# Scores over three PSUM banks, row maxima one step ahead of the gate chunks, and half the value projection ahead of the last attend

## The reference

```python
# L0: attention with 16 heads of 16, then a SwiGLU layer, f32
a = gamma * rmsnorm(x) + beta
q, k, v = a @ W_q.T, a @ W_k.T, a @ W_v.T
attn = softmax(0.25 * q @ k.T); o = attn @ v
x = x + alpha * (o @ W_o.T)
h = gamma2 * rmsnorm(x) + beta2
x = x + alpha2 * (silu(h @ gate_w.T) * (h @ hidden_w.T) @ out_w.T + out_b)
# L1: gated MLP (1024), activations rounded to 8 bits by row, down_w to three values
u = (x * scale * rsqrt(mean(x * x))) @ up_w.T; val, gate = split(u)
x = x + act_quant(val * gelu(gate)) @ weight_quant(down_w).T
# L2: an adapter 256 -> 128 -> 256 whose weights a hyper network makes per sequence
x = x + relu(x @ Wd_b.T + bd) @ Wu_b.T + bu
# L3: layer norm, a per-sequence offset, weight and bias
```

## Time and profile before

| what | value |
|---|---|
| median of 3 runs | 1128.26 us (1128.12 to 1128.39) |
| the profiled execution | 1123.06 us, its span (first to last instruction) 1121.3 us |
| mean granted PE clock over the span | 0.960 |
| a full pass, as pass 8 | 61.9 us |

### The profile page before, as it was taken

The page is one execution under the profiler, slowest core; times in us unless marked ns, Lnnn a source line. Parts: engine busy times, 40 slices in busy tenths (PEclk is TensorE's granted clock), DMA queues, the critical chain, the costliest instruction groups (busy, mean ns, idle before and its releaser), DMA issues.

```text
span 1121.3 us, 22327 instructions
## 1 busy us (share of the span) xinstructions
PE 1006.8 (90%) x7426; PEld 850.9 (76%) x7426; DVE 752.4 (67%) x1711; ACT 553.2 (49%) x1144; POOL 193.1 (17%) x250
## 2 busy tenths in 40 slices
PE   5586789999999999999999999999999999997964
PEld 4245659697988879796979888797979788885952
DVE  4645547686777767776767677777867677776552
ACT  3154354655555454646555554646465545545430
POOL 1421601021120202010111202020201112020210
PEclk9578999999999999999999999999999999999995
DMA  8974622030404021120404040211304040300000
GB/s 292 296 294 133 250 91 66 22 113 2 133 1 127 5 91 41 49 83 6 126 1 132 1 122 10 81 51 39 93 1 132 1 132 1 113 11 10 11 19 9
DMA packets 78049, 89.45 MB, mean 80 GB/s; under 512 B 18672, under 2 KB 64640, under 8 KB 75392
## 3 DMA queue, kind: packets, MB, share of 16 engines
q1 hardware_dynamic: 72368, 63.86, 19.0%
q0 software_dynamic: 2304, 16.78, 4.1%
q10 hardware_dynamic: 3344, 8.39, 2.2%
HBM read 63.14 MB, written 25.31 MB: 79 GB/s over the span
## 4 chain that ended last, share of the span: by engine, by line
PE 69%; DVE 12%; DMA 6%; issue 5%; ACT 4%; SPq 2%; POOL 1%; DVEq 0%; ACTq 0%; POOLq 0%
PE bank L639 15%; PE bank L594 15%; PE bank L555 8%; PE bank L608 5%; PE bank L539 5%; PE bank L565 5%; PE bank L573 3%; DMA q_stack<-few_rows 3%; PE bank L500 2%; PE bank L671 2%; PE bank L657 2%; PE bank L677 1%; DVE den_x L1151 1%; DVE den_x L1153 1%; DVE o_norm L1155 1%
## 5 line engine op out<-in xcount | busy, mean ns | idle before, releaser
L1120 DVE TENSOR_REDUCE neg_max<-bank 128x2 f32<-128x512 f32 x256 | 164.8, 684 | 18.7 <-PE bank L539 18.7
L457 POOL TENSOR_TENSOR act_lo<-act_f,act_hi 128x256 fp32r<-128x256 f32 x128 | 94.4, 738 | 423.7 <-ACT act_hi L907 423.6
L865 ACT ACTIVATE probs<-bank 128x512 f32<-128x512 f32 x256 | 138.4, 593 | 57.1 <-PE bank L555 56.7
L901 ACT ACTIVATE silu_g<-bank 128x256 f32<-128x256 f32 x128 | 49.1, 384 | 183.5 <-PE bank L594 183.3
L555 PE MATMUL bank<-q_stack,k_stack 128*128 128x256 f32 x512 | 106.4, 324 | 9.6 <-DMA q_stack<-few_rows 6.4
L555 PEld LDWEIGHTS bank<-q_stack,k_stack 128*128 128x128 f32 x512 | 75.1, 195 | 50.0 <-ACT probs L865 30.9
L639 PE MATMUL bank<-up_hi,h_hi 128*128 128x256 f32 x512 | 108.0, 292 | 1.7 <-DVE y L1093 1.0
L944 ACT ACTIVATE gelu_g<-bank,r 128x256 f32<-128x256 f32 x128 | 60.7, 474 | 95.7 <-PE bank L639 94.8
L594 PE MATMUL bank<-h_hi,gh_hi 128*128 128x256 f32 x512 | 103.6, 284 | 4.6 <-DVE h_lo L1181 4.6
L594 PE MATMUL bank<-h_lo,gh_hi 128*128 128x256 f32 x512 | 103.4, 284 | 0.0
L639 PE MATMUL bank<-up_lo,h_hi 128*128 128x256 f32 x512 | 102.9, 282 | 0.0
(11 more groups left out here) (158 smaller groups left out, 2127.4 us busy)
## 6 DMA issues: line engine op xcount, KB each, us to landing
hyper<-w_hyper POOLq DMA_DIRECT2D x16, 1024.0 KB, 7.0
q_stack<-q_dram SPq DMA_DIRECT2D x96, 128.0 KB
k_stack<-k_dram SPq DMA_DIRECT2D x96, 128.0 KB
q_dram<-probs SPq DMA_DIRECT2D x16, 512.0 KB, 2.8
k_dram<-probs SPq DMA_DIRECT2D x16, 512.0 KB, 3.6
x_res<-xT SPq DMA_DIRECT2D x16, 256.0 KB, 2.8
out<-xc SPq DMA_DIRECT2D x16, 256.0 KB, 2.5
x_in<-xT SPq DMA_DIRECT2D x15, 256.0 KB, 2.8
```

The costliest lines, as they stand in the source:

```text
L457: pool.tensor_tensor(act_lo[:, c % 3, :], act_f[:, c % 2, :], act_hi[:, c % 3, :].bitcast(F32), ALU.subtract).then_inc(g_lo.sem, 1)
L865: act.activation(probs[:, h % SLOTS], halves(h % 2), ACT.Exp, scale=float(H / D) ** 0.5).then_inc(s_exp.sem, 1)
L1120: dve.tensor_reduce(neg_max[:, qt, :, pair:pair + 1].rearrange("p a o -> p (a o)"), halves(n % 3), AX_X, ALU.max, negate=True).then_inc(ma ...
```

## The change

1. The blocks of `max_scores` are given out by `maxima(c)`: three in step 0, two in each of steps 1 to 6, and the last one behind `ffn_out` in step 6. `max_turn` moves from step 8 to step 7, behind gate 7 and ahead of `ffn_out(f, 5)`. On DVE the reductions follow this, and the last stands ahead of the gated product of step 7. On ACT `max_row_out` moves ahead of the last `act_high`.
2. The scores use banks 0, 1 and 5 in turn, and a score waits for the exponential three heads back. The first three scores follow `mlp_down(g, 0)`, two more the second `mlp_down`, and two go ahead of and behind each `attend` from there; the last one stands alone. The small steps of `g` (`y_turn`, `adapter_down`, `adapter_up`) move from ahead of the scores of each turn to behind its `attend`. `norm_g` moves behind scores 3 and 4 and from bank 5 to bank 3, so the third `attend` waits for its end on DVE. On ACT `square_g` moves behind exponential 1 and `guess_g` from behind exponential 3 to behind 5. On DVE `norm_a(nxt)` goes ahead of `scaled_y(g)`.
3. `project_v(nxt, 0)` moves from behind `ln_var` to ahead of the last `attend`. It waits for `n1_dve` too.

```diff
@@ -33,6 +33,7 @@
 UW = F // UC
 BN = 128
 SLOTS = 7
+SCORE_BANKS = (0, 1, 5)
 NHY, HYW = 16, 2048
 MAGIC = 12582912.0
 EPS_RMS, EPS_LN = 1e-6, 1e-5
@@ -289,6 +290,10 @@
             run(Batch(NB - 1), Batch(NB - 2), Batch(NB - 3), None)
             run(None, Batch(NB - 1), Batch(NB - 2), None)
             run(None, None, Batch(NB - 1), None)
+
+        def maxima(c):
+
+            return range(0, 3) if c == 0 else range(2 * c + 1, 2 * c + 3)
 
         def starts(b):
 
@@ -516,6 +521,7 @@
                         mm.then_inc(done.sem, 1)
 
                 def project_v(b, t):
+                    pe.wait_ge(n1_dve.sem, n1_dve.at(b))
                     if t == 0 and b.follows():
                         pe.wait_ge(o_dve.sem, o_dve.at(b, 5, back=1))
                     for c in range(DC):
@@ -549,10 +555,10 @@
                     if h == 0:
                         pe.wait_ge(max_dma.sem, max_dma.at(b))
                         pe.wait_ge(max_row.sem, max_row.at(b))
-                    if h >= 2:
-                        pe.wait_ge(s_exp.sem, s_exp.at(b, h - 1))
+                    if h >= 3:
+                        pe.wait_ge(s_exp.sem, s_exp.at(b, h - 2))
                     for k in range(TT):
-                        mm = pe.matmul(halves(h % 2)[:, k, :], k_stack[:, h, k * P:(k + 1) * P], q_stack[:, h // 2, :],
+                        mm = pe.matmul(halves(SCORE_BANKS[h % 3])[:, k, :], k_stack[:, h, k * P:(k + 1) * P], q_stack[:, h // 2, :],
                                        start=True, stop=True)
                     mm.then_inc(s_mm.sem, 1)
 
@@ -615,7 +621,7 @@
                     pe.wait_ge(n3_act.sem, n3_act.at(b, 1))
                     for t in range(TT):
                         for c in range(DC):
-                            mm = pe.matmul(bank[5][:, t:t + 1], sq3[:, c, t * P:(t + 1) * P], mean_w[:, 0:1],
+                            mm = pe.matmul(bank[3][:, t:t + 1], sq3[:, c, t * P:(t + 1) * P], mean_w[:, 0:1],
                                            start=(c == 0), stop=(c == DC - 1))
                     mm.then_inc(n3_pe.sem, 1)
 
@@ -718,10 +724,10 @@
                             q_turn(g, 0)
                         if g and c == 6:
                             q_turn(g, 1)
-                        if a and c < FC:
-                            max_scores(a, 2 * c)
-                            max_scores(a, 2 * c + 1)
-                        if a and c == FC:
+                        if a and c < FC - 1:
+                            for n in maxima(c):
+                                max_scores(a, n)
+                        if a and c == FC - 1:
                             if starts(a):
                                 pe.wait_ge(small_in.sem, 16 * 6)
                             max_turn(a)
@@ -731,40 +737,43 @@
                             norm_a(nxt)
                         if f and c >= 2:
                             ffn_out(f, c - 2)
+                        if a and c == FC - 2:
+                            max_scores(a, 15)
                         if starts(a) and c in (7, 9):
                             hyper_product(c // 2 - 1)
                         if starts(f) and c in RUN1:
                             hyper_product(8 + RUN1.index(c))
                     if g:
                         mlp_down(g, 0)
-
                     if a:
-                        scores(a, 0)
-                        scores(a, 1)
+                        for h in range(0, 3):
+                            scores(a, h)
                     if g:
                         mlp_down(g, 1)
+                    if a:
+                        for h in range(3, 5):
+                            scores(a, h)
                     if f:
                         norm_g(f)
-                    if a:
-                        scores(a, 2)
-                        scores(a, 3)
                     for t in range(4):
-                        if g and t < 3:
-                            (y_turn, adapter_down, adapter_up)[t](g)
                         if a:
+                            if t == 2 and f:
+                                pe.wait_ge(n3_dve.sem, n3_dve.at(f))
                             if t < 3:
-                                scores(a, 4 * t + 4)
                                 scores(a, 4 * t + 5)
-                            if t == 2 and f:
-                                pe.wait_ge(x2_dve.sem, x2_dve.at(f))
+                                scores(a, 4 * t + 6)
+                            elif nxt:
+                                project_v(nxt, 0)
                             attend(a, t)
-                            if t < 3:
-                                scores(a, 4 * t + 6)
-                                scores(a, 4 * t + 7)
                         if starts(a):
                             hyper_product(4 + t)
                         if starts(f) and t >= 2:
                             hyper_product(12 + t)
+                        if g and t < 3:
+                            (y_turn, adapter_down, adapter_up)[t](g)
+                        if a:
+                            for h in range(4 * t + 7, min(4 * t + 9, H)):
+                                scores(a, h)
 
                     if nxt:
                         project_qk(nxt)
@@ -776,7 +785,7 @@
                         project(a)
                     if g:
                         ln_var(g)
-                    if nxt:
+                    if nxt and not a:
                         project_v(nxt, 0)
                     if a:
                         norm_f(a)
@@ -862,7 +871,7 @@
                         act.wait_ge(qk_dram_w.sem, qk_dram_w.at(b))
                     if h >= SLOTS:
                         act.wait_ge(pv_mm.sem, pv_mm.at(b, (h - SLOTS) // 4 + 1))
-                    act.activation(probs[:, h % SLOTS], halves(h % 2), ACT.Exp, scale=float(H / D) ** 0.5).then_inc(s_exp.sem, 1)
+                    act.activation(probs[:, h % SLOTS], halves(SCORE_BANKS[h % 3]), ACT.Exp, scale=float(H / D) ** 0.5).then_inc(s_exp.sem, 1)
 
                 def den_guess(b, u):
                     act.wait_ge(o_dve.sem, o_dve.at(b, 8 * u + 3))
@@ -916,7 +925,7 @@
                     act.wait_ge(n3_pe.sem, n3_pe.at(b))
                     if b.follows():
                         act.wait_ge(n3_dve.sem, n3_dve.at(b, back=1))
-                    act.activation(y3[:], bank[5][:, 0:TT], ACT.Ln, bias=eps_rms).then_inc(n3_act.sem, 1)
+                    act.activation(y3[:], bank[3][:, 0:TT], ACT.Ln, bias=eps_rms).then_inc(n3_act.sem, 1)
                     act.wait_ge(n3_act.sem, n3_act.at(b, 2))
                     act.activation(y3[:], y3[:], ACT.Exp, scale=-0.5).then_inc(n3_act.sem, 1)
 
@@ -993,17 +1002,15 @@
                             square_a(nxt)
                         if f and c == 2:
                             bias_x1(f)
+                        if a and c == FC:
+                            max_row_out(a)
                         if f and c >= 1:
                             act_high(f, c - 1)
                         if starts(f) and c in RUN1:
                             hyper_out_piece(8 + RUN1.index(c))
-                    if a:
-                        max_row_out(a)
                     act.preload_act_table_set("natural_log_exp_and_others")
                     if nxt:
                         guess_a(nxt)
-                    if f:
-                        square_g(f)
                     if starts(a):
                         hyper_out_piece(3)
                         raw_load(3)
@@ -1014,7 +1021,9 @@
                         for h in range(4 * t, 4 * t + 4):
                             if a:
                                 exps(a, h)
-                            if f and h == 3:
+                            if f and h == 1:
+                                square_g(f)
+                            if f and h == 5:
                                 guess_g(f)
                             if f and h == 9:
                                 hi_g(f)
@@ -1199,7 +1208,7 @@
                                                  ALU.mult, ALU.add).then_inc(x2_dve.sem, 1)
 
                 def norm_g(b):
-                    v = bank[5][:, 0:TT]
+                    v = bank[3][:, 0:TT]
                     dve.wait_ge(n3_act.sem, n3_act.at(b))
                     dve.scalar_tensor_tensor(v, v, EPS_RMS, y3[:], ALU.add, ALU.mult).then_inc(n3_dve.sem, 1)
                     dve.wait_ge(n3_dve.sem, n3_dve.at(b, 1))
@@ -1315,14 +1324,13 @@
                         dve.wait_ge(consts.sem, 6)
                         dve.wait_ge(ternary.sem, TERNARY)
                     for c in range(FC):
-                        if f and c < FC - 1:
+                        if a and c == FC - 1:
+                            row_max(a, 15)
+                        if f:
                             gated(f, c)
-                        if a:
-                            row_max(a, 2 * c)
```

(10 more changed lines are left out.)

## The result

The changed kernel takes 1105.05 us (median of 4 runs, 1103.09 to 1106.64) beside 1128.19 us before (4 runs): a ratio of 0.9831, 95% interval 0.9801 to 0.986. The prediction said 1097.6, between 1087 and 1112. Its profiled execution took 1104.08 us with a span of 1102.3; the span before was 1121.3. So 19.0 us went from the span, where the sum by steps had 30.7.

What follows compares the result with a forecast made beforehand. PE, busy 90% of the span, was taken to bound the kernel. 1.8 us in each of 14 full passes, 5 in pass 1 and 0.5 in pass 0 gave 30.7: 1092.4, plus 5.2 for the median: 1097.6, range 1087 to 1112.

Steps and rivals of the forecast that it cites:

- the sum by steps: Whole kernel: 1.8 us in each of 14 full passes, 5 in pass 1, 0.5 in pass 0, in all 30.7 us.
- two rivals: Third bank brings nothing (1108.8 us, chance 0.15); DVE's lag from the early maxima reaches gates and `ffn_out` (1111.6, chance 0.13).
- Maxima one step ahead: PE ahead of the row maxima's transposes and first scores: first scores start 1.0 us earlier a pass, bounds 0.5 to 1.1.
- The 0.95 at the transposes: PE hole ahead of the row maxima's transposes, waiting for the last score block's reduction; claimed to go, 0.95 us.
- Scores over three banks: Score stretch: last score starts 11.5 us after the first instead of 12.14, gaining 0.6 a pass, bounds 0 to 1.1.
- the shorter tail: End of the score stretch: last exponential ends 1.1 us after its score starts instead of 1.33, 0.2 more a pass.
- The rival that the third bank brings nothing: Score stretch: ACT keeps the pace, a pass gains 1.0 us, 19.5 in all, giving 1108.8; chance 0.15.
- the prediction's own signs of being wrong: Gates waiting for `act_f`, last exponential no earlier against the first, or a clock under 1.00 between 200 and 980 us.
- small waits: Score stretch before the change: 1.1 of its 13.53 us, taken as PE waiting for exponentials, seen in a pair taking 0.91.
- The value projection: Half of it moved ahead of the last attend, off the path: 0 us; rival counting 0.86 in 13 passes, 1086.4, chance 0.07.
- The clock: Full passes: forecast to stay at 1.00; rival: new hole before `norm_f` lets it fall each pass, 1139.6 us, chance 0.05.
- Pass 1: First scores idle 3.90 us for the row's DMA, then clock 0.50: gain 5 us, between 2 and 7; first exponential near 134.4.

## Why the prediction was right, and where it was off

- **The time: in the range, in part by luck.** A full pass gained 1.22 us where 1.8, give or take 0.4, was forecast, and the span lost 11.7 us less than the sum said. The time is only 7.45 off, because the 5.2 between the median and the profiled execution of the kernel before was added, and here it was 0.97. With the sum's error alone the time would have been 1109.3, in the part of the range that had been added for two rivals.
- **Maxima one step ahead: right, and worth 1.30 where 1.0 was forecast, at most 1.1.** DVE's slack was there: the gated product of step 6 comes at 554.93 after 0.89 us of idle, where the earlier trace rows had 0.98, and the page's group of the reductions has no idle time ahead of it. The 0.95 at the transposes went. The other 0.35 is the wait of the first scores for the DMA of the row: they start 0.86 behind the first `mlp_down` now (560.86 to 561.72), which is nearly all its own work (the second takes 0.80), and started 1.22 behind it before (571.06 to 572.28). The prediction took that wait at the 0.17 of the bracket in the earlier trace rows, and a record's end lies behind the time at which PE is free. The copy of the row also came 1.3 earlier, not 1.1: it starts 37.68 behind the `project` of the pass before (558.41), where it started 38.97 behind it.

```profile
554.93 0.42 DVE L1196 TENSOR_TENSOR act_f<-bank,silu_g 128x256 f32<-128x256 f32 x1 [0.89 <-ACT silu_g L910]
...
558.24 0.42 DVE L1196 TENSOR_TENSOR act_f<-bank,silu_g 128x256 f32<-128x256 f32 x1 [1.09 <-ACT silu_g L910]
```

```profile
L1129 DVE TENSOR_REDUCE neg_max<-bank 128x2 f32<-128x512 f32 x256 | 161.9, 681 | 0.0
```

- **Scores over three banks: 0.8 forecast (0.6 and the shorter tail), -0.08 measured.** This is the step that failed. It misses 0.88 us a pass, 12.3 over 14 passes, of which the maxima gave back 4.2. The rival that the third bank brings nothing comes nearest to the time (1108.8), but not for its reason: ACT did not keep the pace, it waited for scores. The last score starts 12.27 behind the first (561.72 to 573.99), where 11.5 was forecast and 12.14 stood before. And one of the prediction's own signs of being wrong came: the last exponential ends no earlier against the first, 12.95 us behind its start (562.34 to 575.29) in place of 12.77. Two terms of the sum failed. First, the sums of PE (11.3) and of ACT (10.5) were compared over the stretch, and what matters is how long ACT gets nothing at a time; moving the small steps behind the attends made these gaps longer. PE then waits at two scores, 10 and 14, some 0.45 each (the bracket and the 0.16 by which a record ends late), where one wait of 0.3 was forecast. Three scores ahead of the attend gave back 0.69, close to the 0.8 of the forecast. Second, a pair of scores was taken at 0.58 and the rest of 0.91 called a wait. With three banks and no wait in the profile a pair between an adapter product and an attend still takes 0.75 (562.30 to 563.05). So not all of the 1.1 us that the prediction called small waits in the old order was one. The third bank takes 0.6 of it: 0.26 ahead of the pair behind `y_turn` (0.61 from the start of `y_turn` at 575.12 to the 575.73 of the earlier trace rows, and 0.35 from 558.95 to 559.30 with three banks) and 0.17 within each of two pairs (0.91 at 575.73, now 0.75). 0.20 was the wait for `x`, and the rest is work. In the changed kernel the 16 scores hold PE for about 5.1 us (0.81, 0.66, 0.64, 0.79, 0.44, 0.89, 0.43 and 0.42, the 0.79 and 0.89 being records less their 0.16), not 4.64.
- **What DVE does in front of the small steps: missed.** The prediction looked at `norm_a` only for `y_turn` and found cover. The prices are 0.28 and 0.70 us a pass in the old order. The new order hides it by having the steps late, where they starve ACT; with the steps early in it, `y_turn` waited 0.73.
- **The value projection: right**, 0.01 and 0.02 us a pass in two pairs of kernels, and for the reason given: the path does not run through that attend. Its signs came as forecast: `attend(3)` without a wait at 575.37, 0.93 (1.1 forecast) ahead of `norm_f` released by ACT's square, and 0.51 (0.6) ahead of `project`.
- **The clock: right that it holds in a full pass.** It stood at 1.00 in every full pass, with holes of 0.93 and 0.51 in each. The swings of which the Trainium skill tells (TensorE: Matmul & The Clock Gate, "A second HAM failure mode: psum-queue depth-cycling") did not show. What the same page of the Trainium skill reports of its own kernel ("HAM oscillation — how this bites in real kernels"), that one more PSUM buffer gave nothing, is not so here: 0.22 us a pass in the old order and 1.70 in the new.
- **Pass 1: 5 forecast, 1.9 measured.** The transposes gained 0.1 there (127.95 to 127.86) and not the hole: the clock was 0.50 between 103 and 105, where it was 0.88 before, and a hyper product then waited 1.11 us for its load. (The kernel with three banks in the old order has the same three blocks in its first step, and its clock was 1.00 over the same two us.) The 3.90 of the earlier trace rows went, and 2.09 of idle for an exponential came at 136.41; the first exponential starts at 135.76, not near 134.4. The clock fell all the same, to 0.50 from 137 on. In the kernel before it fell at about the same time (1.00 up to 137.5, 0.60 from there to 138, then 0.50); the earlier trace rows start behind that fall:

```profile
118.67 1.06 PE L706 MATMUL bank<-hyper,cond_t 128*32 128x512 f32 x8 [1.11 <-DMA hyper<-w_hyper]
...
136.41 1.29 PE L561 MATMUL bank<-q_stack,k_stack 128*128 128x256 f32 x4 [2.09 <-ACT probs L874]
```

  Moving the hyper piece halved PE's idle time there (1.02 in place of 2.09) and pass 1 was no shorter, which speaks against ACT's queue. It is not settled, since each pass 1 here is that of one execution. What decides when the clock falls stays open: pass 1 took from 64.67 us at a mean clock of 0.94 to 71.27 at 0.82 over the kernels tried, and pass 0 from 86.8 to 92.2, but the kernel before by itself took from 1117.7 to 1131.3 us in its executions. How much of the spread is the kernel's and how much the execution's was not tried.

## What to carry to other kernels

Where one engine feeds another through a few buffers, sum the work between two deliveries, not only the work of the stretch: here the consumer starved in the longest gaps, and a further buffer gave most where the order ran the producer several scores in a row. Before an order is called bound by a buffer, look which operands of the same stretch another engine makes late; one swap on DVE, which adds no work, nearly tripled what the third bank gave (0.22 to 0.64). And test an order with and without the resource it was made for: this one costs 1.78 us a pass with two banks and 0.30 with three, so the kernel with the old order, the third bank and `residual_3` first is the faster one (1089.67 us).

## What was not expected of the hardware

- A pair of scores takes 0.57 us between starts with an attend ahead of it and an adapter product behind it (561.05 to 561.62), and 0.75 the other way round (562.30 to 563.05), with no wait recorded in either; an attend uses tiles of 128x32 in place of 128x128. In the changed kernel the pair between `norm_g` and an attend takes 0.64 (564.91 to 565.55), so what stands ahead counts as well as what stands behind. A single score ahead of the value projection takes 0.42 (573.99 to 574.41), in a pair 0.29. Whether the change of shape is what costs was not tried by itself.
- With all the same loads to do, pass 1 lies 6.6 us apart between single executions of kernels that differ in the order of a few instructions, and so does its mean clock, 0.82 to 0.94.
